# A four-layer graph network on one core: moving set-up work between the first stage and the adjacency build

## The chip, the cores and the metric

The kernel runs on one core of a Trainium2 chip. The metric is the device time of one execution in microseconds; of several timed runs the median counts. A core has TensorE (PE, with its weight loads shown as PEld), VectorE (DVE), ScalarE (ACT), GpSimd (POOL), which here issues the gathers, and SyncE (SP), which issues the other transfers. Each engine works through its own list of instructions in order, and they wait for each other through semaphores.

## The reference

Four layers of a graph network on 6250 nodes with 128 features and 106250 directed edges, sorted by target, each followed by a residual and a layer norm:

```python
edge_index = jnp.stack([src, dst])
x = _layernorm(x + L0(x, edge_index, edge_attr_64, ...))   # messages by a two-layer MLP, then a GRU
x = _layernorm(x + L1(x, edge_index, ...))                 # GCN on src, dst, their reverse and loops
x = _layernorm(x + L2(x, edge_index, ...))                 # GCN with loops, PReLU
x = _layernorm(x + L3(x, src, dst, edge_weight, ...))      # three GCN convolutions with edge weights
```

What the change touches belongs to layer 0, `segment_sum(relu([x[src], edge_attr] @ W1.T + b1) @ W2.T + b2, dst)` with a GRU behind it, and to the tables of edges that all layers use.

## The kernel before

Nodes are padded to 49 blocks of 128. Edges lie in tiles of 128 partitions and T = 832 columns, four columns to a step (208 steps). The program runs in blocks with a barrier of all engines between them.

The **first stage** (0 to 57 us) loads edges, nodes and weights, multiplies x by the node part of layer 0's first weight, and stores the result as `p_table` in 13 groups of four blocks: PE multiplies, ScalarE evicts, SP stores in four pieces. VectorE meanwhile derives one column per property of an edge: target block, row in the block, source pair, three bf16 parts of the weight (ScalarE casts them in two splits between its evictions, `SPLIT_BEFORE`), the first target of each step, and the flags of the "low" blocks: `near_low` (an edge that the first blocks' sparse path handles), `kept[q]` (not to be used for the low set q, with 16 or 24 blocks), `low_local[q]` and `low_first[q]`. It also splits the GRU's bias rows into three bf16 planes (`add_row`, `add_part`), in turn with ScalarE. At the end SP copies the planes row by row into `deg_w`, nine transfers.

The **build** (58 to 1389 us) does two things at once, in 49 rounds u, one per target block. First, it makes dense count and weight matrices: VectorE sorts the edges of a block (`sort_keys`, `sort_ranks`, `sort_out`) and writes one-hots of source and target in two halves h of 14 and 12 slots (`one_hots`); from round 16 on (`NARROW`) it also writes three weighted copies. PE multiplies the one-hots (`blocks`), ScalarE evicts, SP stores. Second, it computes layer 0's messages, 208 steps spread over the rounds: POOL gathers `p_table` rows, four gathers a step, into a ring of 8 steps (L951); PE multiplies the edge attributes (`edge_part`); VectorE adds the two (L711) and writes a 64-wide one-hot (L707); ScalarE applies the relu; PE sums two steps by target (`sum_part`, L883); VectorE adds that to `acc` (L719, L720).

The order is fixed by hand. A place is a point of PE's list, 7 to a narrow round and 13 to a wide one; `at_place` says which step falls on a place. PE runs `edge_part` and `sum_part` there (`first_layer`); VectorE's `tick` handles the step 5 places later in narrow rounds and 8 in wide ones, counted in its own list, which runs ahead of PE's; ScalarE 4 and 6. L707 waits for an earlier sum, since it writes over the one-hot which that sum read. POOL waits for L711 of the step eight back.

Of the kernel before, what the change touches and what calls it, by code (L numbers as in the profile page):

```python
# [20 lines left out]
P = 128  # L21
N = 6250
E = 106250
FD = 128
ED = 64
HID = 256
NB = (N + P - 1) // P
# [3 lines left out]
T = STEPS * TS  # L31
TR = -(-T // P) * P
TH = 4
W = 64
# [106 lines left out]
def build(nc, a, out):  # L141
    with ExitStack() as ctx:
# [36 lines left out]
        left_sum = nc.dram_tensor("left_sum", [P, 2, NP], F32).ap()  # L179

# [19 lines left out]
        low_local = [sb(f"low_local{q}", [P, n * TH]) for q, n in enumerate(low_steps)]  # L200
# [41 lines left out]
        with ExitStack() as c:  # L242
# [14 lines left out]
            with ExitStack() as c0:  # L257
# [21 lines left out]
                in_low = sb("in_low", [P, T], F32, c0)  # L279
# [5 lines left out]
                first_low = sb("first_low", [1, low_steps[0]], F32, c0)  # L285
# [15 lines left out]
                add_in, add_split, add_out = sem("add_in"), sem("add_split"), sem("add_out")  # L301
                XQ = 4
                SPLIT_BEFORE = (5, 9)
# [4 lines left out]
                with nc.Block() as block:  # L308
                    @block.sync
                    def _(sp):  # L310
# [8 lines left out]
                        for to, name in ((wihT, "wihT"), (w2, "w2"), (b2r, "b2r")):  # L319
                            sp.dma_start(to[:], a[name]).then_inc(weights_in, 16)  # L320
# [23 lines left out]
                    def _(pool):  # L344
                        nc.gpsimd.iota(iota_i[:], [[1, 2 * P]], base=0, channel_multiplier=0).then_inc(iotas, 1)
                        nc.gpsimd.iota(row_i[:], [[1, 1]], base=0, channel_multiplier=1).then_inc(iotas, 1)
                        pool.wait_ge(iotas, 2)

                    @block.scalar
                    def _(act):  # L350
# [7 lines left out]
                        for q, (j, n) in enumerate(PG):  # L358
                            if q in SPLIT_BEFORE:
# [6 lines left out]
                        act.wait_ge(wmul_done, 1)  # L366
                        nc.scalar.copy(wcT[:], ps_w[:, 0, 0:3 * FD])
                        nc.scalar.copy(add_row[:, 0, 0:3 * FD], ps_w[0:1, 1, 0:3 * FD]).then_inc(add_in, 1)
                        act.wait_ge(add_in, 2)
                        nc.scalar.copy(add_part[:, 0], add_row[:]).then_inc(add_split, 1)  # L370
                        act.wait_ge(add_in, 3)
# [4 lines left out]
                    def _(dve):  # L376
# [15 lines left out]
                        chain.step(V.memset(add_row[:, 0, 3 * FD:], 0.0))  # L392
# [1665 lines left out]
```

## Time and profile before

| | us |
|---|---|
| median of three timed runs (lowest, highest) | 4200.97 (4194.10, 4204.69) |
| profiled execution, its own time | 4185.11 |
| its span (first to last instruction) | 4183.3 |
| first stage, to the first gather | 58.3 |
| build, to the start of the block behind it | 58.3 to 1389.5 |

| engine | busy us of the span |
|---|---|
| PE | 3684.5 (88%) |
| POOL | 2631.0 (63%) |
| DVE | 2600.4 (62%) |
| ACT | 1519.8 (36%) |

These shares are means over stages with different limits. In a timeline each line has the start, the duration, the engine, the line of the program, and output and inputs by name; in brackets stands the idle time ahead of it and what ended it. A wait names the instruction that waited and the one that released it. Names of transfers lead from destination to source. The granted clock is the share of full speed that PE was given.

### The profile page before, as it was taken

What the parts mean: (1) busy time and instruction counts of PE and PEld (TensorE: products, weight loads), DVE (VectorE), ACT (ScalarE), POOL (GpSimd) and SP (SyncE); (2) the same over time, 40 slices, a digit from 0 to 9 for tenths busy, and PEclk for the clock granted to TensorE, in tenths of its full rate; (3) what the DMA queues carried; (4) which work ended last, traced back from release to release, by engine and by line L of the source; (5) the groups of instructions that cost most, each with busy time, mean ns of one, the idle gap of its engine ahead of it and who ended that gap; (6) DMA issues with size and microseconds to landing.
All of it is one profiled execution on the core that took longest, in us unless ns stands there. A gap on an engine that the chain in (4) does not pass through costs nothing. (4 is left out here: it accounts for less than half of the span.)

```text
span 4183.3 us, 80810 instructions
## 1 busy us (share of the span) xinstructions
PE 3684.5 (88%) x30230; PEld 2456.0 (59%) x30230; DVE 2600.4 (62%) x5064; ACT 1519.8 (36%) x3170; POOL 2631.0 (63%) x2363
## 2 busy tenths in 40 slices
PE   5889999999999637888878869999799899989998
PEld 4778888888888523444444435554545555544444
DVE  8888888777777575555533344664366566514665
ACT  3445777776667440000000003332244344303332
POOL 3888788788786016566367747774476566407773
PEclk6778999999999869999989989999899999989999
DMA  4556888888888369999767758998565555529997
GB/s 152 152 147 201 285 284 282 287 278 262 272 269 270 135 202 310 311 317 315 256 217 239 237 162 314 323 328 295 168 216 194 184 194 189 181 87 326 328 323 254
DMA packets 612893, 1019.38 MB, mean 244 GB/s; under 512 B 90889, under 2 KB 417576, under 8 KB 612112
## 3 DMA queue, kind: packets, MB, share of 16 engines
q1 hardware_dynamic: 476700, 773.91, 54.0%
q0 software_dynamic: 90848, 199.74, 16.2%
q10 hardware_dynamic: 44956, 40.55, 3.0%
q8 instruction: 243, 3.98, 0.4%
q14 instruction: 146, 1.19, 0.1%
HBM read 737.12 MB, written 276.78 MB: 242 GB/s over the span
## 5 line engine op out<-in xcount | busy, mean ns | idle before, releaser
L951 POOL DMA_INDIRECT x<-p_table,src_i x832 | 1029.0, 1237 | 310.4 <-issue 242.1
L1541 POOL DMA_INDIRECT rows_b<-x_table,low_src x552 | 575.4, 1042 | 485.4 <-POOLq L159 206.7
L1541 POOL DMA_INDIRECT rows_a<-h_table,low_src x412 | 451.4, 1096 | 231.8 <-issue 121.3
L1620 PE MATMUL po_l3b<-mat_l3b,rows_b 128*128 128x512 f32 (+1 forms) x1372 | 575.7, 567 | 20.2 <-DMA mat_l3b<-weights_fwd 19.2
L930 ACT CAST st_cnt<-ps_mat 128x512 bf16<-128x512 f32 (+1 forms) x825 | 443.1, 596 | 294.4 <-PE ps_deg L845 284.5
L1620 PE MATMUL po_l3a<-mat_l3a,rows_a 128*128 128x512 f32 (+1 forms) x882 | 375.4, 573 | 29.2 <-DMA mat_l3a<-weights_fwd 28.4
L1620 PE MATMUL po_l3c<-mat_l3c,rows_a 128*128 128x512 f32 (+1 forms) x882 | 375.3, 573 | 15.6 <-DMA mat_l3c<-weights_fwd 14.8
L1620 PEld LDWEIGHTS po_l3b<-mat_l3b,rows_b 128*128 128x128 f32 x1372 | 242.9, 196 | 244.6 <-issue 223.4
L1620 PE MATMUL po_l<-mat_l,rows_a 128*128 128x512 bf16 (+1 forms) x1323 | 291.6, 376 | 100.1 <-DVE mat_l L1860 99.3
L860 PE MATMUL ps_mat<-rows_a,hot_s 128*128 128x128 bf16 x4851 | 346.9, 221 | 8.9
L1541 POOL DMA_INDIRECT rows_a<-x_table,low_src x276 | 286.2, 1037 | 93.1 <-issue 84.2
L1775 ACT ACTIVATE t_l<-y_l 128x512 f32<-128x512 f32 (+1 forms) x26 | 15.7, 605 | 886.7 <-DVE y_l L1915 886.7
L1541 POOL DMA_INDIRECT rows_a<-m_table,low_src x276 | 278.2, 1008 | 92.3 <-issue 81.3
L843 PE MATMUL ps_mat<-hot_s,rows_a 128*128 128x256 bf16 x1225 | 317.8, 280 | 0.0
L1620 PE MATMUL po_l<-mat_l,rows_b 128*128 128x512 bf16 (+1 forms) x1323 | 289.6, 373 | 18.9 <-DMA mat_l<-counts_fwd 18.1
L860 PEld LDWEIGHTS ps_mat<-rows_a,hot_s 128*128 128x128 bf16 x4851 | 277.9, 98 | 46.2 <-ACT st_wt L935 36.5
L841 PE MATMUL ps_deg<-slots,hot_s 128*128 128x1 bf16 x2401 | 278.5, 166 | 13.5 <-issue 7.6
L840 PE MATMUL ps_mat<-rows_a,hot_s 128*128 128x128 bf16 x1617 | 248.5, 220 | 26.6 <-DVE rows_a L699 12.2
L1620 PEld LDWEIGHTS po_l<-mat_l,rows_a 128*128 128x128 bf16 x1323 | 123.2, 102 | 240.6 <-DVE mat_l L1860 113.8
L1620 PEld LDWEIGHTS po_l3a<-mat_l3a,rows_a 128*128 128x128 f32 x882 | 158.8, 198 | 174.8 <-issue 145.1
L1728 ACT ACTIVATE split_l3b<-rows_a,low_weight 128x256 bf16<-128x256 f32 x412 | 175.4, 496 | 216.8 <-DMA rows_a<-h_table,low_src 149.4
L1620 PEld LDWEIGHTS po_l3c<-mat_l3c,rows_a 128*128 128x128 f32 x882 | 158.0, 198 | 160.7 <-issue 145.1
(419 smaller groups left out, 7207.2 us busy)
## 6 DMA issues: line engine op xcount, KB each, us to landing
weights_fwd<-st_wt SPq DMA_DIRECT2D x396, 256.0 KB
mat_l<-counts_fwd SPq DMA_DIRECT2D x112, 896.0 KB
mat_l3a<-weights_fwd SPq DMA_DIRECT2D x56, 1792.0 KB
mat_l3c<-weights_fwd SPq DMA_DIRECT2D x56, 1792.0 KB
counts_rev<-st_cnt SPq DMA_DIRECT2D x588, 128.0 KB
rev_l<-counts_rev SPq DMA_DIRECT2D x84, 896.0 KB, 10.8
mat_l3b<-weights_fwd SPq DMA_DIRECT2D x42, 1792.0 KB
counts_fwd<-st_cnt SPq DMA_DIRECT2D x396, 128.0 KB
```

The lines of the kernel that those rows point to most:

```text
L840: nc.tensor.matmul(ps_mat[:, b, q * P:(q + 1) * P], half, rows, start=True, stop=True)
L841: nc.tensor.matmul(ps_deg[:, 2 * k + q:2 * k + q + 1], half, slots[:, u % 2, NV, k, 0:1], start=False, stop=False)
L843: nc.tensor.matmul(ps_mat[:, b, rev_at:rev_at + len(halves) * P], rows, hot_s[:, h, j0 + j, 0:len(halves) * P], start=True, stop=True)
L860: mm = nc.tensor.matmul(ps_mat[:, f % 3, (2 * j + q) * P:(2 * j + q + 1) * P], half, hot_w[:, h, v, j0 + j, :], start=(v == 0), stop=(v == 2))
L930: nc.scalar.copy(st_cnt[:, q, :, j * 2 * P:j * 2 * P + n_col], ps_mat[:, f % 3, :].rearrange("p (d c) -> p d c", d=2)[:, :, 0:n_col]).then ...
L951: pool.indirect_dma_start(ring[:, j % RING, t * FD:(t + 1) * FD], None, p_table, bass.IndirectOffsetOnAxis(src_i[:, j * TH + t:j * TH + t ...
L1541: pool.indirect_dma_start(ring[:, j % RL, t, :], None, table, bass.IndirectOffsetOnAxis(low_src[:, j * TH + t:j * TH + t + 1].bitcast(U32), 0)
L1620: mm = nc.tensor.matmul(po[:, p % 2, k, 0:nb * P].rearrange("p (d c) -> p d c", c=P), rows[:, s, k * P:(k + 1) * P], cols, start=(s == 0 a ...
L1728: part = nc.scalar.activation(split[:, j % 2, 0, t, :], ring[:, j % RL, t, :], ACT.Copy, scale=low_weight[:, j * TH + t:j * TH + t + 1])
L1775: nc.scalar.activation(t1[:, 0:nb, 0:FD], y2[:, f % ys, 0:nb], ACT.Square).then_inc(act_out, 1)
```

## The change

Four things are changed.

- The flags of the low blocks are no longer made in the first stage. Only the shifted target block is left there, in `near_low`; sixteen VectorE instructions (`low_flags`) make the rest in rounds 2 to 8 of the build, in the bf16 tiles. `low_local` is one tile for both sets. The one-hots' second half has 11 slots instead of 12.
- The bias planes are made by ScalarE and POOL instead of ScalarE and VectorE; the weight product behind them is moved ahead of PE's third group, its weights ahead of x in SP's queue, and ScalarE's steps between the evictions. One transfer stores all planes in memory; three transfers of the build load `deg_w` from there.
- ScalarE's splits come one group later, VectorE's second one earlier.
- `sum_part` runs at the place behind the one where it ran.

The core of the diff, with equal parts left out:

```diff
-                SPLIT_BEFORE = (5, 9)
+                SPLIT_BEFORE = (6, 10)
...
                         sp.dma_start(w1xT[:], a["w1xT"]).then_inc(w1x_in, 16)
+                        for to, name in ((wihT, "wihT"), (w2, "w2"), (b2r, "b2r")):
+                            sp.dma_start(to[:], a[name]).then_inc(weights_in, 16)
                         for q in range(XQ):
...
                         sp.wait_ge(add_split, 3)
-                        for r in range(9):
-                            sp.dma_start(deg_w[r:r + 1, :], add_part[:, r % 3, r // 6, :]).then_inc(add_out, 16)
-                        sp.wait_ge(add_out, 16 * 10)
+                        sp.dma_start(deg_terms.rearrange("v k c -> (v k c)").unsqueeze(0), add_part.rearrange("o v k c -> o (v k c)")
+                                     ).then_inc(add_out, 16)
+                        sp.wait_ge(add_out, 16 * 2)
...
+                        pool.wait_ge(gru_in, 48)
+                        nc.gpsimd.tensor_tensor(add_row[:, 1, 0:2 * FD], add_row[:, 1, 0:2 * FD], gb[:], ALU.add).then_inc(add_in, 1)
+                        pool.wait_ge(add_split, 1)
+                        nc.gpsimd.tensor_tensor(add_row[:], add_row[:], add_part[:, 0], ALU.subtract).then_inc(less_part, 1)
+                        pool.wait_ge(add_split, 2)
+                        nc.gpsimd.tensor_tensor(add_part[:, 2], add_row[:], add_part[:, 1], ALU.subtract).then_inc(add_split, 1)
...
                         for q, (j, n) in enumerate(PG):
+                            if q == 2:
+                                act.wait_ge(wmul_done, 1)
+                                nc.scalar.copy(wcT[:], ps_w[:, 0, 0:3 * FD])
+                                nc.scalar.copy(add_row[:, 0, 0:3 * FD], ps_w[0:1, 1, 0:3 * FD]).then_inc(add_in, 1)
+                            if q == 4:
+                                act.wait_ge(add_in, 3)
+                                nc.scalar.copy(add_part[:, 0], add_row[:]).then_inc(add_split, 1)
                             if q in SPLIT_BEFORE:
...
+                        act.wait_ge(less_part, 1)
                         nc.scalar.copy(add_part[:, 1], add_row[:]).then_inc(add_split, 1)
...
-                        chain.step(V.tensor_copy(tmp_f[:], tmp_i[:]))
-                        dve.wait_ge(gru_in, 48)
-                        V.tensor_tensor(add_row[:, 1, 0:2 * FD], add_row[:, 1, 0:2 * FD], gb[:], ALU.add).then_inc(add_in, 1)
...
-                            chain.step(V.tensor_copy(low_first[q][:], first_low[:]))
-
-                        dve.wait_ge(add_split, 2)
-                        V.tensor_tensor(add_part[:, 2], add_row[:], add_part[:, 1], ALU.subtract).then_inc(add_split, 1)
+                        chain.step(V.tensor_copy(near_low[:], tmp_i[:]))
                         dve.wait_ge(begin_done, 1)
...
+                            if q == 1:
+                                pe.wait_ge(weights_in, 16 * 3)
+                                nc.tensor.matmul(ps_w[:, 0, 0:3 * FD], w2[:], wihT[:], start=True, stop=True)
+                                nc.tensor.matmul(ps_w[:, 1, 0:3 * FD], b2r[:], wihT[:], start=True, stop=True).then_inc(wmul_done, 1)
...
+                    def low_flags(u):
+
+                        n = low_steps[1] * TH
+                        if u == 2:
+                            chain.step(V.scalar_tensor_tensor(out=kept[1][:].rearrange("p (h t) -> p h t", t=TH),
+                                                              in0=near_low[:].rearrange("p (h t) -> p h t", t=TH),
+                                                              scalar=-float(PER_GROUP), in1=per_row(iota_256[:, 0:HS], TH),
+                                                              op0=ALU.mult, op1=ALU.add))
+                            chain.step(V.tensor_scalar(kept[0][:], kept[1][:], -float(EARLY_BY), None, ALU.is_ge))
+                        if u == 3:
+                            chain.step(V.scalar_tensor_tensor(out=kept[1][:], in0=kept[1][:], scalar=float(LATE_BY), in1=kept[0][:],
+                                                              op0=ALU.is_lt, op1=ALU.mult))
+                            chain.step(V.tensor_scalar(kept[0][:], local0[:], float(W), None, ALU.is_lt))
+                        if u == 4:
+                            chain.step(V.tensor_reduce(total[:, 3:4], kept[0][:], AX.X, ALU.add))
+                            chain.step(V.tensor_tensor(near_low[:], kept[1][:], kept[0][:], ALU.mult))
...
-                        n = 2 * HALF if h == 0 else NK + 1 - 2 * HALF
+                        n = 2 * HALF if h == 0 else NK - 2 * HALF
...
                             sort_keys(u + 2)
+                        low_flags(u)
                         tick()
...
-                        e = at_place.get(place(u, s))
-                        if e is not None:
-                            if e < HS:
-                                edge_part(e)
-                            if e >= 4 and e % 2 == 0:
-                                sum_part((e - 4) // 2)
+                        at = place(u, s)
+                        if at is None:
+                            return
+                        e = at_place.get(at)
+                        if e is not None and e < HS:
+                            edge_part(e)
+                        e = at_place.get(at - 1)
+                        if e is not None and e >= 4 and e % 2 == 0:
+                            sum_part((e - 4) // 2)
...
                     edges(1)
+                    for r in range(3):
+                        sp.dma_start(deg_w[3 * r:3 * r + 3, :], deg_terms[:, r // 2, :]).then_inc(terms_in, 16)
...
+                    sp.wait_ge(terms_in, 48)
                     sp.wait_ge(nodes_in, 16)
```

Rounds 5 to 8 of `low_flags` hold ten more instructions: a reduction, a comparison, a comparison and a scaled sum on 412 columns, two scaled comparisons for `kept[1]` and `kept[0]`, and four on one partition for `low_first`.

## Rows read from the trace of the kernel before

**Rows 1.** Waits of SP's queue, 0 to 62 us: us, times, longest.
```profile
SPq L338 <- DVE diag L483: 12.1, 1, 12.1
SPq L308 <- DMA deg_w<-diag: 1.0, 1, 1.0
```

**Rows 2.** Timeline of SP, first stage: start, us, operation, count.
```profile
50.36 5.69 SPq L338 DMA_DIRECT2D deg_w<-diag  x9
```

**Rows 3.** Timeline of POOL: first gather, last gather, a copy behind the build.
```profile
58.32 1.10 POOL L951 DMA_INDIRECT x<-p_table,src_i  x1 [57.04 <-POOLq L308]
...
1339.73 0.94 POOL L951 DMA_INDIRECT x<-p_table,src_i  x1 [0.32 <-issue]
...
1370.33 2.12 POOL L957 COPY rows_a<-dst_i 128x832 int32<-128x832 int32 x1
```

**Rows 4.** Timeline of VectorE, first stage.
```profile
27.79 2.48 DVE L443 TENSOR_TENSOR vals<-tmp_f,src_f 128x832 bf16<-128x832 f32 x1
...
37.94 0.59 DVE L460 CAST near_low<-tmp_f 128x832 bf16<-128x832 f32 x1
...
42.66 1.01 DVE L468 SCALAR_TENSOR_TENSOR src_f<-dst_blk,same 128x832 f32<-128x832 bf16 x1
...
49.12 1.21 DVE L483 TENSOR_TENSOR diag<-add_row,diag 1x1024 bf16<-1x1024 f32 x1
```

**Rows 5.** Groups by line, POOL: count, busy, mean ns, idle before.
```profile
L951 POOL DMA_INDIRECT x<-p_table,src_i x832 | 1029.0, 1237 | 310.4 <-issue 242.1 <-POOLq L308 57.0 <-DVE x L711 11.3
```

**Rows 6.** Waits of VectorE, 58 to 1370 us.
```profile
DVE x L711 <- DMA x<-p_table,src_i: 54.2, 34, 5.0
DVE hot_s L688 <- PE ps_mat L860: 28.8, 16, 4.1
DVE hot L707 <- PE pa L883: 12.2, 11, 2.4
```

**Rows 7.** Stretches: us; PE, PEld, DVE, ACT, POOL busy; clock; DMA share, GB/s.
```profile
378.00:858.00 480.00, 468.61 (x6527) 425.82 (x6528) 397.31 (x700) 344.88 (x694) 384.85 (x313) 1.00 0.88 283
858.00:1338.00 480.00, 457.44 (x6202) 416.51 (x6199) 372.79 (x660) 328.70 (x660) 383.65 (x317) 0.97 0.85 271
```

**Rows 8.** Timelines of POOL, then VectorE, 353 to 378 us.
```profile
361.52 1.76 POOL L951 DMA_INDIRECT x<-p_table,src_i  x1 [0.31 <-issue]
...
373.78 1.12 POOL L951 DMA_INDIRECT x<-p_table,src_i  x1 [0.30 <-issue]
...
360.45 2.02 DVE L688 TENSOR_TENSOR hot_s<-iota,slots 128x3584 bf16<-128x3584 bf16 x1
...
364.85 0.68 DVE L711 TENSOR_TENSOR x<-pm,x 128x512 f32<-128x512 f32 x1
```

**Rows 9.** Timelines of PE, then ScalarE, first stage.
```profile
13.99 6.62 PE L505 MATMUL ps_p<-w1xT,x 128*128 128x128 f32 x56
...
23.92 6.48 PE L505 MATMUL ps_p<-w1xT,x 128*128 128x128 f32 x32 [3.31 <-ACT rows_a L364]
...
20.84 2.51 ACT L362 CAST vals<-tmp_w 128x832 bf16<-128x832 f32 x1 [1.44 <-DVE tmp_w L428]
23.03 1.22 ACT L364 COPY rows_a<-ps_p 128x512 f32<-128x512 f32 x2
...
40.38 1.04 ACT L370 CAST diag<-add_row 1x1024 bf16<-1x1024 f32 x1
```

**Rows 10.** Transfers, first stage: count, KB each, us to landing.
```profile
p_table<-rows_a SPq DMA_DIRECT2D x1, 576.0 KB, 3.5
```

**Rows 11.** Groups by line and shape, VectorE, 58 to 1400 us.
```profile
L688 DVE TENSOR_TENSOR hot_s<-iota,slots 128x3584 bf16<-128x3584 bf16 x49 | 99.3, 2027 | 32.6 <-PE ps_mat L860 28.2 <-PE ps_deg L845 4.2
...
L688 DVE TENSOR_TENSOR hot_s<-iota,slots 128x3072 bf16<-128x3072 bf16 x49 | 86.0, 1756 | 1.6 <-PE ps_mat L860 0.7
```

**Rows 12.** Timeline of PE, 1343 to 1347 us.
```profile
1343.58 1.95 PE L883 MATMUL pa<-hot,x 128*128 128x64 f32 x16
...
1345.97 0.83 PE L860 MATMUL ps_mat<-rows_a,hot_s 128*128 128x128 bf16 x12
```

More of the change, by code:

```diff
@@ L391, in _ @@
                         chain.step(V.memset(ones_b[:], 1.0))
-                        chain.step(V.memset(add_row[:, 0, 3 * FD:], 0.0))
+                        V.memset(add_row[:, 0, 3 * FD:], 0.0).then_inc(add_in, 1)
                         chain.step(V.tensor_scalar(col_f[:], row_f[:], float(P), None, ALU.mult))
@@ L451, in _ @@
-                        V.tensor_tensor(add_row[:, 1, 0:2 * FD], add_row[:, 1, 0:2 * FD], gb[:], ALU.add).then_inc(add_in, 1)
-                        chain.step(V.tensor_copy(src_f[:].rearrange("p (h t) -> p h t", t=TH), per_row(iota_256[:, 0:HS], TH)))
-                        chain.step(V.scalar_tensor_tensor(out=tmp_f[:], in0=tmp_f[:], scalar=-float(PER_GROUP), in1=src_f[:],
-                                                          op0=ALU.mult, op1=ALU.add))
-                        chain.step(V.tensor_scalar(src_f[:], tmp_f[:], -float(EARLY_BY), None, ALU.is_ge))
@@ L456, in _ @@
-                        chain.step(V.scalar_tensor_tensor(out=tmp_f[:], in0=tmp_f[:], scalar=float(LATE_BY), in1=src_f[:],
-                                                          op0=ALU.is_lt, op1=ALU.mult))
-                        chain.step(V.tensor_scalar(in_low[:], local0[:], float(W), None, ALU.is_lt))
-                        chain.step(V.tensor_tensor(tmp_f[:], tmp_f[:], in_low[:], ALU.mult))
-                        chain.step(V.tensor_copy(near_low[:], tmp_f[:]))
-                        chain.step(V.tensor_reduce(near_sum[:], tmp_f[:], AX.X, ALU.add))
@@ L678, in sort_out @@
                                         ALU.is_gt).then_inc(slots_ready, 1)
+                    def low_flags(u):
[13 more added lines that the diff above has]
+                            chain.step(V.tensor_tensor(near_low[:], kept[1][:], kept[0][:], ALU.mult))
+                        if u == 5:
+                            chain.step(V.tensor_reduce(near_sum[:], near_low[:], AX.X, ALU.add))
+                            chain.step(V.tensor_scalar(kept[0][:], pair2[:], float(2 * NK), None, ALU.is_equal))
+                        if u == 6:
+                            chain.step(V.tensor_tensor(kept[1][:, 0:n], near_low[:, 0:n], kept[0][:, 0:n], ALU.is_le))
+                            chain.step(V.scalar_tensor_tensor(out=low_local[:], in0=kept[1][:, 0:n], scalar=FAR,
+                                                              in1=local0[:, 0:n], op0=ALU.mult, op1=ALU.add))
+                        if u == 7:
+                            chain.step(V.scalar_tensor_tensor(out=kept[1][:], in0=dst_blk[:], scalar=float(LOWS[1]), in1=kept[0][:],
+                                                              op0=ALU.is_ge, op1=ALU.max))
+                            chain.step(V.scalar_tensor_tensor(out=kept[0][:], in0=dst_blk[:], scalar=float(LOWS[0]), in1=kept[0][:],
+                                                              op0=ALU.is_ge, op1=ALU.max))
+                        if u == 8:
+                            chain.step(V.tensor_scalar(low_first[1][:], first_i[:, 0:low_steps[1]], LAP - 1, None, ALU.bitwise_and))
+                            chain.step(V.tensor_copy(first_low[:], first_i[:, 0:low_steps[0]]))
+                            chain.step(V.tensor_scalar(first_low[:], first_low[:], float(LOWS[0] * P), None, ALU.min))
+                            chain.step(V.tensor_copy(low_first[0][:], first_low[:]))
```

51 lines of the change are left out of this document (12 added, 39 removed).

## The prediction

> **What bounds the kernel now.** The change touches the first stage (0 to 57 us) and the build (58 to about 1389 us), so I read those two and leave the layers behind them alone. First the SP queue's waits, to see what ends the first stage: SP stands 12.1 us at the bias planes until VectorE's last subtraction has made them, then issues nine transfers and waits 1.0 us more [rows 1]. The nine take 50.36 to 56.05, the first gather of the build starts at 58.32 [rows 2, 3]. VectorE's chain shows why they are late: the source column is done at 30.27, and nearly all between there and 49.12 is low-block flags [rows 4]. So the first stage ends with VectorE, and then with SP.
>
> Then the build. POOL issues 832 gathers: busy 1029.0 us, and of the 310.4 us of gaps 57.0 lie ahead of the first one; the other 253.4 make 0.30 us for each [rows 5]. So POOL is never held by anything: 1282.4 us from 58.32 to 1340.67 [rows 3]. VectorE waits 54.2 us for landed gathers, in 34 places [rows 6], so late in the build the messages run at the gathers' pace. PE agrees: in the first half of the wide part it is busy 468.61 of 480 us at clock 1.00, in the second half 457.44 at 0.97 [rows 7]. The gather stream is what bounds the build, and **whatever lets it begin earlier, or shortens it, shortens the kernel**.
>
> What stretches a gather? Most rows show 0.94 us, the mean is 1.237 us [rows 5]. The one at 361.52 took 1.76: it began while the one-hot comparison L688 (360.45 to 362.47) ran, and ended 0.81 us after it [rows 8]. I matched all 832 by start and end: 388 are longer than 0.96, and all but one of them ended about 0.82 us after a VectorE instruction that was running when they began. Together that is 1029.0 - 832 x 0.943 = 244 us. The blockers all read two tiles in SBUF.
>
> The Trainium skill says the same of the cause (GPSIMD Engine Reference, section 1, Specifications): POOL's SBUF interfaces are shared with VectorE, with contention from instructions that have two SBUF inputs or run in a 2-port mode. It speaks against the change in one point: most flag instructions that move beside the gathers have two SBUF inputs. By that rule they would cost the stream some 2 us, by the rows 0 to 3 (below).
>
> **First stage, part by part.** VectorE loses everything from L451 to L483 except one cast. Its chain ends so: L443 ends at 30.27 [rows 4], the second split, moved ahead of it, adds its 1.1; L448's shift and a cast to bf16, 0.6 each [rows 4], and the copy of the block starts: about 33. It ends nothing any more.
>
> ScalarE takes over. PE's first two groups end at 13.99 + 2 x 0.95 = 15.9 (28 blocks in 6.62 us are 0.95 for a group of four [rows 9]). The weight product, now behind them, is four instructions of 384 columns: 12 x 0.118 = 1.4 us at the pace of that row, 12 x 0.2 = 2.4 at the pace of the row at 23.92, where the clock was reduced. PE comes from work here, so I take 1.5: 17.4. It needs its three weights, which now land ahead of x. No row shows x's first part landing; PE took it at 13.99 straight behind other work, so I put the delay at nothing (1 to 2 us if x was only just there). ScalarE then: two copies, 0.5 each, 18.4; two evictions of 0.6 [rows 9], held by PE to 19.9; the first cast, 1.04 [rows 9], 20.9 (it waits for POOL's bias addition, whose inputs must have landed: an open point); groups 4 and 5, 22.1; a split of 2.5 [rows 9], 24.6; groups 6 and 7, 25.8; groups 8 and 9 at PE's slow pace (16 blocks in 6.48 us, 1.62 a group [rows 9]), 29.1; the second split, 31.6; groups 10 and 11, 32.8; the last one, 33.3; the second cast, 34.4.
>
> Now the part that gets dearer: the last subtraction is POOL's. VectorE took 1.21 us for it [rows 4]; the nearest POOL row, a copy of 832 columns, took 2.12, so 2.6 for 1024 [rows 3]. Ends 1.2 and 2.6; I take 2.4, nearer to POOL's own row: 36.8. SP issues one transfer instead of nine, 0.6 [rows 2], 37.4. Its landing is bounded by 1.0 us [rows 1] and 3.5 (the shortest store of the p table [rows 10]); I take 2.0, since it writes memory as that one does, but 6 KB and not 576: 39.4. The last p-table store, issued at 33.7, is down by 37.3. From there to the first gather I keep the 1.3 us of before (57.05 to 58.32): **40.7 instead of 58.3, a gain of 17.6 us**, 13 to 20 by the bounds. The three bias-plane transfers that follow stand behind two edge loads in SP's queue and ahead of stores that need PE's first products, many us later; the new wait on them is at the end of the build, 1.3 ms behind: no cost.
>
> **Build, part by part.** (1) Flags. Some sixteen VectorE instructions in rounds 2 to 8. Durations from L468, 1.01 for 832 columns with a scalar and two tensors, and L460, 0.59 for a one-input pass [rows 4]: four of the first kind and two reductions, taken like them, 6.1 us; six lighter or shorter ones 3.5; four of one partition 0.8: 10.4, with the gaps between steps about 11 us of VectorE. (2) One slot less in the second half of each round's one-hots. L688 costs 2.027 for 14 slots and 1.756 for 12 [rows 11]: 0.136 a slot, and 0.07 for each instruction of half that width: 0.2 us a round in 16 narrow rounds, 0.4 in 33 wide ones.
>
> What do they do to the gathers? Every one of the 48 L688 of the second half that ran beside gathers held one, so ending it 0.136 us sooner gives 48 x 0.136 = 6.5 us; 59 of 96 products L699 held one (59 x 0.07 = 4), L691 8 of 48 (0.5). High end 11; low end 0, if the gathers then only run into the next instruction. The flags take back 0 to 3: about seven instructions of 0.6 to 1 us, each blocking perhaps 0.3. Net: **8 us shorter**, 0 to 11.
>
> (3) The ring. POOL may run 8 steps ahead of VectorE. The tightest place I found is step 50: its gather starts at 373.78, VectorE's addition that frees its place ended at 365.53 [rows 8]: 8.2 us of reserve. VectorE will be late by 11 - 16 x 0.2 = 7.8 us there, POOL early by some 2.5. So POOL is held by about 2 us; 0 if PE's own waits hide some of the flags, 10 if they come out twice as dear. A lag that stays under the reserve costs nothing, since VectorE has 54.2 us of waits to give up later [rows 6].
>
> (4) Sums one place later. PE's sum (1.95 us) then ends behind the next place's products: 1345.53 becomes 1346.80, 1.27 later [rows 12]. VectorE waits for these sums ahead of L707, today 12.2 us in 11 places of 104 sums [rows 6]. In the PE-bound part the wait grows, but VectorE has 28.8 us of waits for PE at L688 there [rows 6] that shrink instead. PE itself shows next to no idle ahead of the sums, so there is little to gain: 0, with 0 to 10 us of loss inside the ring's bound above.
>
> Is PE next? With the stream 8 us shorter and VectorE 8 us later, 16 us of the reserve go. PE's loss to waiting in the second half of the wide part is 468.61 - 457.44 = 11 us idle and 3% of 480 us, 14, of clock [rows 7]: 25 us. It stays just behind the gathers.
>
> Sum: -17.6 - 8 + 2 = **-23.6 us**. The profiled execution took 4185.1 (span 4183.3); that is 16 below the median of the timed runs, 4201.0, which lie between 4194.1 and 4204.7. I put the difference on the median: 4201.0 - 23.6 = 4177.4, for the profile a span near 4160.
>
> **Rivals.** A: the first stage gains but the stream doesn't shorten, since a gather freed from one instruction meets the next; 244 us of blocking then stays as it is: -17.6 + 2 = 4185. For it: the blockers stand back to back. Against: the release follows the end of the blocker.
> B: the ring closes. The flags and the later sums put VectorE 20 us behind instead of 8, POOL is held for some 12 us, and PE becomes the bound: -17.6 + 12 - 4 = 4191, within 0.3%. For it: a reserve of 8.2 us only. Against: the reserve grows later, and PE's waits take some of the flags.
> C, the slower one: the later sums bind VectorE everywhere. 104 sums x 1.27 = 132 us; VectorE's waits can take 54.2 + 28.8 = 83 of it, 49 stay: -17.6 + 49 = +31, 4232. It decides once nearly every sum is waited for; today 12 of 104 are.
> D: the change does less than it says: the bias rows land late (they follow x in SP's queue), ScalarE stands ahead of group 4, and all evictions behind it move. Seen in the rows only as an upper bound: they were there by VectorE's addition at 32.6. Then the first stage gains 6 instead of 17.6: 4189, within 0.3%.
>
> The Trainium skill also weighs on the POOL step (GPSIMD Engine Reference, section 3.1): two-input elementwise work runs about half as fast on POOL as on VectorE, 4497 ns for 2048 columns. An estimate from it is 2.25 us for 1024; the sum would move by 0.2 us.
>
> **Chances.** Forecast 0.60 (own range 4166 to 4184), A 0.20, B 0.10, D 0.06, C 0.04. About 0.3%, 12.6 us, is what a measurement of this kernel can tell from no change. Forecast and A lie beyond it, save for their edges: faster 0.82, the same 0.14, slower 0.04. For 8 in 10 the range takes in the forecast with its bounds, A and most of B: 4162 to 4192.
>
> **What would show it.** First gather at 39 to 42 us in the trace after; VectorE idle at the end of the first stage; ScalarE's last eviction near 33. L951 with a mean of 1.225 to 1.23 us, and a last gather 25 us sooner. POOL held once or twice near round 16, under 3 us. VectorE's waits for landed gathers falling from 54 to about 40. L707's waits for PE's sums rising from 12 to 20 or 30. It is wrong if the gathers' sum of gaps grows by 10 us or more (B), if VectorE's waits for landed gathers vanish (B, C), or if ScalarE stands at group 4 (D).

## The result and the profile of the changed kernel

| | before | changed |
|---|---|---|
| median of five timed runs, us | 4202.66 (4194.10 to 4204.69) | 4171.96 (4160.65 to 4176.94) |
| profiled execution, its span, us | 4183.3 | 4159.8 |
| first gather starts, last one ends | 58.3, 1340.7 | 39.2, 1315.9 |
| gather stream | 1282.4 | 1276.7 |
| PE's end of the build | 1368.7 | 1345.4 |
| from there to the end of the span | 2814.6 | 2814.4 |

The ratio is 0.9943, 95% interval 0.9923 to 0.9964: 0.6% faster. 4177.4 was predicted, with a range of 4162 to 4192. In the profiled executions the span falls by 23.5 us where 23.6 were predicted, and nearly all of it is there at PE's end of the build (23.3). That the two meet so closely is luck; the terms, added up at the end, are off by 1.5 to 2.3 us each and cancel.

First the end of the first stage. Timeline of the changed kernel (start, us, engine, line): ScalarE's second split and last cast, POOL's subtraction, the first and the last gather, and POOL's first copy behind the build, which starts when PE is done; then a row of PE, and SP's.

```profile
29.44 2.50 ACT L374 CAST vals<-tmp_w 128x832 bf16<-128x832 f32 x1 [1.75 <-DVE tmp_w L447]
...
33.10 1.04 ACT L379 CAST diag<-add_row 1x1024 bf16<-1x1024 f32 x1
...
34.22 2.49 POOL L352 TENSOR_TENSOR diag<-add_row,diag 1x1024 bf16<-1x1024 f32 x1 [10.41 <-ACT diag L379]
39.18 1.11 POOL L964 DMA_INDIRECT x<-p_table,src_i  x1 [2.47 <-POOLq L307]
...
1314.93 0.94 POOL L964 DMA_INDIRECT x<-p_table,src_i  x1 [0.30 <-issue]
1345.46 1.68 POOL L969 COPY rows_a<-src_i 128x832 int32<-128x832 int32 x1 [29.59 <-PE ps_deg L926]
...
25.01 3.95 PE L477 MATMUL ps_p<-w1xT,x 128*128 128x128 f32 x32 [0.92 <-ACT rows_a L376]
...
36.73 0.24 SPq L336 DMA_DIRECT2D deg_terms<-diag  x1
...
39.23 0.90 SPq L984 DMA_DIRECT2D deg_w<-deg_terms  x3
```

ScalarE's cast ends at 34.14 and POOL's subtraction at 36.71, where 34.4 and 36.8 were worked out. What [rows 2] showed as nine transfers in 5.69 us is one of 0.24; the three loads from it come behind the edge loads, at 39.23, when the gathers are already running. The next two views are the waits of SP's queue in the first stage and POOL's group of gathers (count, busy us, mean ns, idle before).

```profile
SPq L336 <- POOL diag L352: 2.6, 1, 2.6
SPq L307 <- DMA deg_terms<-diag: 1.0, 1, 1.0
```

```profile
L964 POOL DMA_INDIRECT x<-p_table,src_i x832 | 1023.3, 1230 | 255.9 <-issue 242.7 <-DVE x L720 10.7 <-POOLq L307 2.5
```

Of the 255.9 us of gaps 2.5 lie ahead of the first gather, and the rest is 253.4, to a tenth what [rows 5] gave: the ring never closed. The busy time fell from 1029.0 to 1023.3. Now VectorE's waits from 39 to 1366 us, and PE's two halves of the wide part (us; busy PE, PEld, DVE, ACT, POOL; clock; DMA).

```profile
DVE x L720 <- DMA x<-p_table,src_i: 52.1, 40, 4.0
...
DVE hot L716 <- PE pa L893: 17.8, 18, 2.4
DVE hot_s L697 <- PE ps_mat L870: 9.4, 5, 2.5
```

```profile
359.00:839.00 480.00, 468.28 (x6568) 435.86 (x6567) 391.19 (x703) 351.82 (x699) 385.16 (x312) 0.99 0.89 285
839.00:1319.00 480.00, 453.60 (x6235) 421.81 (x6235) 374.33 (x669) 334.31 (x663) 380.51 (x317) 0.96 0.85 272
```

Beside [rows 6]: the wait for landed gathers stays (54.2 to 52.1), the wait for PE's sums rises (12.2 to 17.8 in 18 places), the one for PE at the one-hots falls (28.8 to 9.4). PE is in the second half where it was in [rows 7]: below full busy time and below full clock (0.96), fed at the gathers' pace.

### The profile page after: what moved, and what is told of

Same layout as the page of the kernel before. It is cut to its first block and busy times, and to the rows that moved or that the text cites. A ratio compares the mean times of both kernels' runs of the same rounds, so it can differ in the third digit from the quotient of the medians.

```text
span 4159.8 us, 80782 instructions
## 1 busy us (share of the span) xinstructions
PE 3679.8 (88%) x30211; PEld 2473.8 (59%) x30230; DVE 2580.8 (62%) x5056; ACT 1529.6 (37%) x3170; POOL 2634.5 (63%) x2366
## 5 line engine op out<-in xcount | busy, mean ns | idle before, releaser
L964 POOL DMA_INDIRECT x<-p_table,src_i x832 | 1023.3, 1230 | 255.9 <-issue 242.7
L1636 PE MATMUL po_l3c<-mat_l3c,rows_a 128*128 128x512 f32 (+1 forms) x882 | 376.3, 574 | 16.4 <-DMA mat_l3c<-weights_fwd 15.6
L850 PE MATMUL ps_mat<-rows_a,hot_s 128*128 128x128 bf16 x1617 | 248.3, 220 | 29.4 <-DVE rows_a L708 23.6
L880 PE MATMUL pm<-w1eT,rows_a 65*128 65x128 f32 x1664 | 254.8, 301 | 4.6 <-DVE x L720 4.6
```

The lines of the kernel that those rows point to most:

```text
L850: nc.tensor.matmul(ps_mat[:, b, q * P:(q + 1) * P], half, rows, start=True, stop=True)
L880: mm = nc.tensor.matmul(pm[:, j % 2, t * FD:(t + 1) * FD], edge[:, i % 2, (h * TH + t) * P:(h * TH + t + 1) * P], w1eT[:], start=True, sto ...
L964: pool.indirect_dma_start(ring[:, j % RING, t * FD:(t + 1) * FD], None, p_table, bass.IndirectOffsetOnAxis(src_i[:, j * TH + t:j * TH + t ...
L1636: mm = nc.tensor.matmul(po[:, p % 2, k, 0:nb * P].rearrange("p (d c) -> p d c", c=P), rows[:, s, k * P:(k + 1) * P], cols, start=(s == 0 a ...
```

## The experiments

Three quantities are compared throughout: the gather stream, PE's end of the build, and the ring's reserve. The last is read at the tightest step as in [rows 8]: the start of a step's first gather less the end of the addition that freed its place. Behind PE's end the same layers take 2813 to 2826 us from execution to execution, so spans don't tell apart a few us there, and PE's end does. Each kernel was profiled once, so the scatter has to come from kernels that share a build. The changed kernel and the three experiments that leave its build as it is have streams of 1276.7, 1278.1, 1278.4 and 1279.2: some 2.5 us is the scatter of a stream. Single quantities scatter more in these four: VectorE's waits for landed gathers come to 40.5, 52.1, 60.4 and 61.1 us, and of the three that start the stream as soon as they can two have a reserve of 4.0 us at its tightest step, step 50, and one has 9.7.

### Is the end of the build tied to the first gather?

```diff
                 def _(pool):
+                    pool.wait_ge(slots_ready, 1)
                     for j in range(HS):
```

> The changed kernel, with one wait more: POOL's first gather waits until VectorE has written the first block's slots, which it does at 51.2 us in the trace of the changed kernel, so the stream starts at about 51.3 instead of 39.2. Theory (the gather stream bounds the build): the stream keeps its 1277 us, the last gather ends 12 us later, at about 1328, and the span grows by 12 us to about 4172. Rival (PE or VectorE bounds the build, and the stream only happens to run beside it): the span stays within 3 us of 4160.

Measured: ratio 0.9943 (0.9922 to 0.9965), stream 1278.4. POOL's waits, then its timeline:

```profile
POOL x L965 <- DVE slots L652: 14.8, 1, 14.8
```

```profile
51.91 1.11 POOL L965 DMA_INDIRECT x<-p_table,src_i  x1 [14.77 <-DVE slots L652]
...
1360.09 1.68 POOL L970 COPY rows_a<-src_i 128x832 int32<-128x832 int32 x1 [29.73 <-PE ps_deg L926]
```

The first gather is 12.7 us later, PE's end 14.6. The delay goes through whole, so the stream sets the end of the build. The timed runs don't show it: the two ratios are equal, with intervals some 18 us wide.

### The one-hots' slot

```diff
-                        n = 2 * HALF if h == 0 else NK - 2 * HALF
+                        n = 2 * HALF if h == 0 else NK + 1 - 2 * HALF
```

The counterpart, on the kernel before, takes the slot away and changes nothing else.

> The changed kernel with 12 instead of 11 slots in the second half of each round's one-hots. Theory (a gather that begins while a VectorE instruction with two SBUF inputs runs waits for its end, so longer instructions stretch the stream): the stream from first to last gather grows from 1276.7 to 1283 to 1288 us, the span by 6 to 11 us. Rival (the stream's length doesn't depend on them, the 5.7 us it got shorter came from elsewhere): stream and span within 2 us of the changed kernel.

> The kernel before with one edit, 11 instead of 12 slots in the second half of each round's one-hots. Theory (shorter instructions hold gathers for less time): the stream shrinks from 1282.4 to about 1275, by 5 to 11 us, and the span as much, 4172 to 4178 against 4183.3; the first gather stays at 58.3. Rival: both within 2 us of the kernel before.

Measured: with the slot put back into the changed kernel, ratio 0.9955 (0.9936 to 0.9975), stream 1293.3, 16.6 longer where 6 to 11 were expected, PE's end 14.0 later. Without it in the kernel before, ratio 0.9971 (0.9957 to 0.9985), stream 1276.6, 5.8 shorter, but PE's end only 0.7 earlier, since 32.6 us instead of 28.1 lay between the last gather and PE's end. The group of gathers of the first of these kernels, then of the second:

```profile
L964 POOL DMA_INDIRECT x<-p_table,src_i x832 | 1039.9, 1250 | 255.8 <-issue 244.5 <-DVE x L720 8.8 <-POOLq L307 2.5
```

```profile
L951 POOL DMA_INDIRECT x<-p_table,src_i x832 | 1023.2, 1230 | 311.0 <-issue 248.2 <-POOLq L308 57.6 <-DVE x L711 5.2
```

The direction holds on both kernels and all of it is in the gathers' own durations. The size of the whole doesn't carry over from one kernel to the other, but that of the shortened instructions does. Matched as in the prediction, the second half's source one-hots held gathers for 52.5 and 51.4 us in the two kernels with 12 slots, and for 44.5 to 46.2 in the eight with 11 whose one-hots are whole; its weighted copies (L699, now L708) went from 30.0 and 27.8 to between 21.9 and 26.3. That is some 11 us in either setting. What wanders is what VectorE's other instructions hold: without the slot it rose by 6 us in the kernel before, and fell by 5.5 in the changed one.

### Sums at their old place

```diff
-                        e = at_place.get(at - 1)
+                        e = at_place.get(at)
```

> The changed kernel with the message sums back at their old place. Theory (the move is worth nothing while the gathers bound the build): last gather and span within 3 us of the changed kernel (1315.9 and 4159.8); VectorE's waits for PE's sums ahead of its one-hots fall from 17.8 to about 12 us. The stretch from the end of the last gather to PE's last product, 29.5 us against 28.1 before, gets 1 us shorter. Rival (the later place lets PE run faster in the wide rounds): VectorE catches up with the gathers later, by ten steps or more, and the span grows by 3 us or more.

Measured: ratio 0.9914 (0.9889 to 0.9940), stream 1281.7 (5.0 longer), PE's end 2.4 later. VectorE's waits:

```profile
DVE hot_s L697 <- PE ps_mat L870: 27.7, 15, 4.1
DVE hot L716 <- PE pa L893: 15.6, 16, 2.4
```

The wait for PE at the one-hots, 28.8 before and 9.4 in the changed kernel, is back. So its fall belongs to the later sums: it is 27.7 to 32.1 us in the three kernels with the old place and 0.6 to 10.7 in the seven with the later one and whole instructions. VectorE first waits for a landed gather at step 99 with the later sums and at step 123 without, which is what the rival said, and the last gather is 4.6 us later without them, where the theory named 3. But in the kernel before with 11 slots, which has the old place, that first wait comes at step 92, and a faster PE isn't shown: it does 4356 matmuls between 380 and 700 us here and 4336 to 4500 in the four kernels with the changed build. For the end of the build the later sums are worth 2.4 us, about the scatter, and the timed ratios don't part.

### VectorE made later on purpose

Two reductions of `low_flags` are repeated six times each, ten more of 1.01 us.

```diff
-                            chain.step(V.tensor_reduce(total[:, 3:4], kept[0][:], AX.X, ALU.add))
+                            for _ in range(6):
+                                chain.step(V.tensor_reduce(total[:, 3:4], kept[0][:], AX.X, ALU.add))
...
```

> The changed kernel with ten repeated reductions of 832 columns in rounds 4 and 5, 1.05 us each: VectorE is 10.5 us later. Reductions have one input, so they hold no gather themselves. Theory (a lag of VectorE is free up to the reserve of the ring, 4.0 us at step 50 in the trace of the changed kernel, and what lies beyond holds POOL for good): POOL is held for about 6 us near step 50, and the span grows by about 6 us. Rival 1 (VectorE has slack there): 0. Rival 2 (VectorE is on the path in the narrow rounds): 10.5 us.

Measured: ratio 0.9925 (0.9896 to 0.9955). POOL's longest hold and the addition that ends it (a gather at step 50; L722 is the addition), then the same gather and its addition in the changed kernel:

```profile
355.82 1.53 POOL L966 DMA_INDIRECT x<-p_table,src_i  x1 [3.02 <-DVE x L722]
...
354.36 0.68 DVE L722 TENSOR_TENSOR x<-pm,x 128x512 f32<-128x512 f32 x1
```

```profile
353.29 0.94 POOL L964 DMA_INDIRECT x<-p_table,src_i  x1 [0.30 <-issue]
...
348.59 0.68 DVE L720 TENSOR_TENSOR x<-pm,x 128x512 f32<-128x512 f32 x1
```

The gather starts 0.78 us after the addition's end. All gaps of the stream come to 259.7 us, 6.4 over the 253.4 of an open ring: 3.5 at step 50, the rest at steps 28, 29 and 43. In the changed kernel the same gather has 353.29 - 349.27 = 4.0 us of reserve. So the ring's limit is where the prediction had put it, in the narrow rounds and hardest at step 50, and the changed kernel stays short of it. PE's end is 11.2 us later. That is near the number of rival 2, but by another path: the hold is the 6 us of the theory, and 5.5 lie in longer gathers, none of which a reduction held.

### The flags in late rounds

```diff
-                        low_flags(u)
+                        low_flags(u - 30)
```

> The changed kernel with the sixteen flag instructions made in rounds 32 to 38 instead of 2 to 8; nothing else. Of before, of the kernel with its old sums and of the changed one the gather streams were 1282.4 us (1276.6 with 11 slots and no flags), 1281.7 and 1276.7, so by difference the flags lengthened it by 5.1. Theory 1 (the flags cost the stream because they make VectorE late in the narrow rounds, where it has no waits to give up): the ring's reserve at step 50 goes from 4.0 back to 11 to 15 us, the stream is 3 to 6 us shorter (1271 to 1274), PE's end of the build 1340 to 1343 instead of 1345.4. Theory 2 (the flags hold gathers wherever they stand): the reserve comes back too, but the stream stays within 2 us of 1276.7 and PE's end within 2 us of 1345.4.

Measured: ratio 0.9927 (0.9912 to 0.9943), reserve 21.4 us at its tightest and 23.5 at step 50, stream 1282.8, PE's end 1352.1. Neither theory: the reserve comes back (more than the 11 to 15 named), but the stream is 6.1 us longer, where one theory wanted it shorter and the other unchanged. The 5.1 us that a difference of two streams had put on the flags aren't theirs: matched to their gathers, the flags themselves hold four in the changed kernel, for 1.2 us in all. My reading, for which there is no run of its own, is that a stream's loss hangs on where each gather meets VectorE, and any edit shifts all later meetings.

### The two steps of the planes

Nine transfers straight from SBUF as before, with the rest of the change:

```diff
-                        sp.dma_start(deg_terms.rearrange("v k c -> (v k c)").unsqueeze(0), add_part.rearrange("o v k c -> o (v k c)")
+                        for r in range(9):
+                            sp.dma_start(deg_w[r:r + 1, :], add_part[:, r % 3, r // 6, :]).then_inc(add_out, 16)
...
```

> The changed kernel with the nine row transfers of the bias planes back at the end of the first stage, in place of the one, and without the three of the build. Theory: nine issues take 5.7 us instead of 0.24, so the first gather begins at 44.6 instead of 39.2, and the span grows by 5.4 us to about 4165. Rival (the issues are hidden beside the last stores of the p table): first gather within 1 us of 39.2.

The last subtraction back on VectorE:

```diff
-                        nc.gpsimd.tensor_tensor(add_part[:, 2], add_row[:], add_part[:, 1], ALU.subtract).then_inc(add_split, 1)
...
+                        V.tensor_tensor(add_part[:, 2], add_row[:], add_part[:, 1], ALU.subtract).then_inc(add_split, 1)
```

> The changed kernel with the last subtraction of the bias planes on VectorE instead of POOL, ahead of VectorE's last shift and cast. In the trace of the changed kernel POOL takes 2.49 us for it (34.22 to 36.71), and VectorE's cast beside it 2.39 instead of 0.59. Theory (it stands last on the path of the first stage): VectorE does it in 1.2 us and the cast in 0.6, SP issues the planes 1.2 us earlier, the first gather begins at 37.9 instead of 39.2, and the span shrinks by 1.2 us. Rival (something else ends the first stage, the p table's last store, say): first gather within 0.3 us of 39.2.

Measured: nine transfers, ratio 0.9932 (0.9907 to 0.9956), first gather 44.1 (4.9 later), PE's end 6.8 later. Subtraction on VectorE, ratio 0.9928 (0.9911 to 0.9945), first gather 37.5 (1.7 sooner), PE's end 2.1 sooner. Timeline of the first, then of the second:

```profile
44.10 1.11 POOL L964 DMA_INDIRECT x<-p_table,src_i  x1 [7.97 <-POOLq L307]
...
36.15 5.69 SPq L337 DMA_DIRECT2D deg_w<-diag  x9
```

```profile
21.27 2.41 DVE L437 CAST src_f<-src_i 128x832 f32<-128x832 int32 x1
...
33.70 1.21 DVE L454 TENSOR_TENSOR diag<-add_row,diag 1x1024 bf16<-1x1024 f32 x1 [0.18 <-ACT diag L377]
...
35.45 0.59 DVE L456 CAST near_low<-tmp_i 128x832 bf16<-128x832 int32 x1
```

From the issue of the planes to the first gather lie 7.95 us with nine transfers (36.15 to 44.10), as in the kernel before (50.36 to 58.32), and 2.45 with one (36.73 to 39.18). So of the first stage's 19.1 us the one transfer is worth 5.5, and the planes' being ready 13.6 us earlier is the rest. VectorE does the last subtraction in 1.21 us, which is 1.3 less than POOL; the other 0.4 of the 1.7 aren't the subtraction's, for ScalarE's cast ahead of it also ended 0.6 us sooner here. First gathers scatter by as much: in five other kernels that leave the changed first stage as it is they start between 38.5 and 39.6.

### Shorter instructions on VectorE

If a gather waits for the end of the VectorE instruction beside which it begins, the same work in two instructions lets it go sooner. The source one-hots and the rank comparison are cut (shown: the second):

```diff
-                        V.tensor_tensor(at_rank[:], num_r[:], per_block(rank_b[:], P),
-                                        ALU.is_equal).then_inc(lots_ready, 1)
+                        for c0 in (0, P // 2):
+                            cs = slice(c0, c0 + P // 2)
+                            ins = V.tensor_tensor(at_rank[:, cs], num_r[:, cs], per_block(rank_b[:], P // 2), ALU.is_equal)
+                        ins.then_inc(lots_ready, 1)
```

> The changed kernel with three VectorE instructions of each round cut in two: the source one-hots of either half (2.0 and 1.6 us) and the rank comparison (1.5 us). The same work, 147 instructions more. Theory (a held gather gets in at the end of the instruction that holds it, and the stream bounds the build): of the 140 us for which these three hold gathers in the changed kernel (54.7, 45.5 and 39.8) about half goes, so the stream alone would be 60 us or more shorter; PE becomes the bound after some 20 to 29 us (it loses 15 us idle and 3 to 4 per cent of 480 us of clock in the second half of the wide rounds), VectorE gets 10 us more work. Span 4140, 4130 to 4150. Rival (the gathers are held by the sum of such work and not by the length of one instruction): stream and span within 3 us of the changed kernel, or some us slower by VectorE's added instructions.

Measured: ratio 0.9823 (0.9806 to 0.9840), median 4126.34. Group of gathers, then the stretches:

```profile
L969 POOL DMA_INDIRECT x<-p_table,src_i x832 | 968.5, 1164 | 269.1 <-issue 244.1 <-DVE x L725 22.6 <-POOLq L307 2.5
```

```profile
359.00:839.00 480.00, 473.52 (x6732) 440.33 (x6732) 400.85 (x768) 359.97 (x716) 380.34 (x327) 1.00 0.90 292
839.00:1279.00 440.00, 432.92 (x6150) 401.87 (x6148) 368.12 (x699) 329.74 (x657) 344.34 (x300) 1.00 0.91 291
```

The second of these stretches in the changed kernel:

```profile
839.00:1279.00 440.00, 417.33 (x5768) 388.22 (x5768) 343.39 (x613) 308.81 (x613) 351.26 (x292) 0.97 0.86 275
```

VectorE's wait and POOL's copy with the cut instructions:

```profile
DVE x L725 <- DMA x<-p_table,src_i: 6.9, 5, 2.8
```

```profile
1302.22 1.68 POOL L974 COPY rows_a<-src_i 128x832 int32<-128x832 int32 x1 [27.46 <-PE ps_deg L931]
```

The gathers take 54.8 us less, POOL is held 13.2 us by the ring, the stream is 41.5 shorter and PE's end 43.2 earlier, where 20 to 29 were expected before PE would bind. So the blocking is real and can be removed in part at 0.15 us of VectorE for a cut one-hot (2 x 1.08 us against 2.02), and PE had more to give than the 25 us that I had thought: here it is busy over 98% at clock 1.00 from 359 to 1279 us, which it was in neither half of the changed kernel.

Two more on top: the planes' subtraction on VectorE with the flags in late rounds, and then the spreading product cut as well.

> Three edits together on the changed kernel: the source one-hots and the rank comparison in two instructions each (alone: stream 1235.2 us, PE's end 1302.2), the last subtraction of the bias planes on VectorE (alone: first gather 37.5), and the flags in rounds 32 to 38. In the kernel with the cut instructions alone POOL was held 13.2 us by the ring in the narrow rounds, and PE was busy 236.7 to 237.0 of each 240 us from 360 us on, so there PE bounds what follows. Theory (the narrow rounds are VectorE's, and without the flags it runs them about 8 to 11 us sooner): POOL is held for 0 to 4 us, the stream is 1222 to 1230 us, PE's end 1291 to 1297, a span near 4113 to 4122. Rival (PE bounds all of the build there, also the narrow rounds): first gather 2 us sooner, PE's end 1299 to 1302 and the span within 4 us of 4126.

> The former kernel with the product that spreads the slots (2600 columns, 1.50 us; 31 held gathers for 35 us in the wide rounds where the others were cut) in two instructions too. Theory (PE is now the bound behind the narrow rounds): the gathers get shorter by 10 to 20 us in sum, but POOL waits for the ring instead, its gaps grow by about as much, and PE's end is within 3 us of the former kernel's. Rival (the gathers still bound the build): PE's end falls by 8 us or more.

Measured: the first, ratio 0.9794 (0.9778 to 0.9810), median 4114.45, stream 1235.1, PE's end 1301.3. In the profile the rival was right: POOL is still held 11.5 us, moving the flags away from the narrow rounds didn't free it, and PE's end moves by 0.8 us, as the first gather does by 1.0. The timed runs speak for the theory: the median is 12 us under that of the cut instructions alone, where the rival had 4, but the intervals of the two ratios overlap. That stays open. The second, ratio 0.9789 (0.9775 to 0.9803), median 4111.02, stream 1227.5:

```profile
L972 POOL DMA_INDIRECT x<-p_table,src_i x832 | 969.7, 1165 | 272.4 <-issue 239.1 <-DVE x L728 18.7 <-POOLq L307 14.6
```

```profile
1293.84 1.68 POOL L977 COPY rows_a<-src_i 128x832 int32<-128x832 int32 x1 [27.58 <-PE ps_deg L934]
```

Neither theory: the gathers' busy time stays (970.3 to 969.7), the hold falls from 11.5 to 4.4 us, and PE's end is 7.6 sooner. The cut product did hold less, 16.4 us instead of 38.6, but other instructions took all of it back. (The 35 us named above are those of all 49 in the kernel with the cut instructions; the 31 in the wide rounds held 21 of them.) Why the ring holds less there isn't settled; the two timed ratios don't part. Both kernels beat the changed one by about 1.5% (0.9794 and 0.9789 against 0.9943).

## Why the prediction was right, and where its terms were off

- **The bound**: right. A delay of the first gather goes through to PE's end (12.7 and 14.6), and the gain of the whole change is there (23.3). A shorter stream alone was not seen to go through as cleanly: without the slot in the kernel before, 5.8 us of stream gave 0.7 at PE's end.
- **First stage**: 17.6 forecast, 19.1 measured. The chain came as worked out to POOL's end (36.8 and 36.71). The term that was mis-sized lies behind it: 0.6 for the issue, 2.0 for the landing and 1.3 to the gather were 3.9; the trace has 0.24, 1.0 and about 1.2, together 2.47. I had taken 2.0 for the landing, between 1.0 and 3.5, because it writes memory; the lower bound, the same queue's own wait in [rows 1], was it. PE's later groups came at 0.99 us each (four in 3.95, row at 25.01, granted clock 1.00) where I had 1.62, but ScalarE then waited 1.75 us for VectorE's second split, and the two nearly cancel. VectorE did not end at 33 but at 37.4, see below; that ends nothing, as forecast.
- **Bias rows (rival D)**: excluded. POOL's first addition starts at 17.6, when its inputs have landed, well ahead of ScalarE's first cast at 20.1.
- **Stream**: -8 for the slot and the flags together, +2 for the ring; -5.7 measured, with no hold. The mean gather is 1.230 us, the upper edge of what was named. By matched gathers the terms were well sized: the shortened instructions hold some 11 us less, the high end of what was worked out, and the flags hold 1.2 where 0 to 3 were named. The stream as a whole is another matter: the slot was worth 5.8 and 16.6 us in two settings, since what the other instructions hold moves by some us with any edit. A scatter of this size has to be added to such a term's range.
- **Rival A** (no shortening) is not borne out by the net, nor by the slot in either setting. Its mechanism, a gather let go from one instruction that meets the next, is at work all the same: with the cut instructions the three that were cut hold 50.5 us instead of 140.0, and the others took back 35 of these 90. One small reading behind it was wrong: of the 387 matched blockers 385 read two tiles in SBUF, two are copies with one input (L649, 0.1 us in all).
- **Ring (rival B)**: didn't close. Forecast was a hold of 2 us, from 8.2 - 7.8 - 2.5; measured is a reserve of 4.0 at the same step 50. The term that was mis-sized is the gain from the slot: 9.9 us of reserve on the kernel before (8.2 to 18.1) instead of the 3.2 that 16 rounds of 0.2 us give. From there to the changed kernel with its old sums (6.5) it falls by 11.6, where flags and earlier start were worked out as 11 and 2.5. These sizes are loose: two kernels with the same build differ by 5.7 us at this step, and in the changed kernel the slot works the other way, with a reserve of 11.1 with it and 4.0 without.
- **Sums one place later**: 0 forecast, and at the end of the build 2.4 in its favour, about the scatter. Waits for PE's sums went to 17.8, a little under the 20 to 30 named. Rival C falls: 18 of 104 sums are waited for, not all.
- **Waits for landed gathers**: about 40 forecast, 52.1 measured. The step said that VectorE gives up waits as it is made late by flags; but it first waits for a gather at step 99, earlier than before (115). With 40.5 to 61.1 us in the kernels of the same build, a fall to 40 could decide nothing.
- **PE as the next bound**: the conclusion held, PE stays behind the gathers, but its number put the first half at nothing, with no harm to the sum. "25 us" was 11 idle and 14 of clock in the second half alone. With cut instructions PE gave up 43.2 us against the changed kernel: x6150 against x5768 matmuls in 839 to 1279 us is some 27 us at 14 a us, x6732 against x6568 in 359 to 839 some 12. In the first half I had read 468.6 of 480 at clock 1.00 [rows 7] as full; 473.5 can be had. Where PE is starved in short gaps, its busy share says little of what it could do.

Added up at PE's end, the first stage gave 19.1 where 17.6 were forecast and the stream 5.7 where 6 were (8 less a hold of 2 that didn't come), while PE ended 1.5 us later behind the last gather than before (29.52 against 28.05), which was not in the forecast: 23.3 in all. The profiled difference (23.5) and that of the medians (30.7) part by 7 us: the profiled execution of before was 17.6 under its median, that of the changed kernel 10.4.

## What to carry to other kernels

Find the stream that sets the end, and ask what one of its items waits for at its start. Here it was the instruction that another engine had under way, so that instruction's length, and not its engine's load, was the price: cutting two kinds of instructions in two gave more (1.2%) than the whole change had (0.6%). Before you name the next bound, take it from a run in which the present one is loosened, since a starved engine looks nearly full in its busy share.

## What the runs showed of the hardware

**POOL holds VectorE too.** Two casts of VectorE in the first stage took four times their length. Timeline of the changed kernel, VectorE, then POOL's first subtraction:

```profile
21.85 2.41 DVE L439 CAST src_f<-src_i 128x832 f32<-128x832 int32 x1
...
34.14 0.59 DVE L454 TENSOR_SCALAR tmp_i<-dst_i 128x832 int32<-128x832 int32 x1
34.77 2.39 DVE L455 CAST near_low<-tmp_i 128x832 bf16<-128x832 int32 x1
...
21.23 2.58 POOL L350 TENSOR_TENSOR add_row<-add_row,diag 1x1024 f32<-1x1024 f32 x1 [2.90 <-ACT diag L370]
```

In the kernel before the cast of `src_f` took 0.59, as did that of `near_low` [rows 4]. Both began after a subtraction of POOL had begun (21.23 and 34.22) and ended 0.45 us after its end (23.81 and 36.71). With the second subtraction on VectorE, the cast of `near_low` took 0.59 again, and the first one 2.41 still. The first of the two made VectorE's second split late, and so ScalarE's wait of 1.75 us. POOL was held as well: its subtraction at 34.22 began while VectorE's shift ran (34.14 to 34.73) and ended 1.98 us after it, so part of its 2.49 us, at most 0.5, was waiting. In all eight kernels where POOL does this subtraction, its end lies 1.97 to 1.98 us after that of the shift.

The Trainium skill has a rule that fits both directions (SBUF — State Buffer, section "SBUF: two separate sides"): VectorE and POOL have a pair of ports in common as an exclusive lock; of a POOL instruction and one of VectorE that runs in a 2-port mode or, where POOL's reads SBUF, has two SBUF inputs, whichever starts first keeps it for its whole instruction, and the other stands still. These rows agree, on POOL's side with one-partition subtractions; in which mode the casts run no row shows. The other rows do too: in the kernel before, all 49 gathers that began beside a rank comparison (two SBUF inputs) were held, and none of the 57 that began beside the addition L711, which reads PSUM and SBUF. The 0.45 us of a cast and the 0.82 us of a gather behind the end of the blocker are 0.12 to 0.14 less than either takes unheld (0.59 and 0.94).

**What an instruction blocks goes by its length.** With the rank comparison whole (1.49 us) the 49 of them lengthened gathers by 39.8 us in the changed kernel; cut (0.82 us), its pieces did so by 13.8. The first half of the source one-hots went from 54.7 to about 24, with some work of holding passed to others: the target one-hots (L700), which come right behind them and were not cut, went from 13.1 to 41.3, the spreading product, behind the rank comparison, from 20.1 to 35.4; the weighted copies L708 fell from 53.3 to 44.0. These are sums over gathers matched by start and end, each as its duration less 0.943 us.
